# Filler matmuls at three places of each group in the attention layer of a two-layer graph network

## What is computed

```python
s_u = x @ W_u.T + b_u
s_v = x @ W_v.T
e = s_u[src] + s_v[dst]
e = jnp.where(e >= 0, e, 0.2 * e)
m = jax.ops.segment_max(e, dst, num_segments=n_nodes)
e_exp = jnp.exp(e - m[dst])
denom = jax.ops.segment_sum(e_exp, dst, num_segments=n_nodes)
msg = xh[src] * (e_exp / denom[dst])[:, None, :]
out = jax.ops.segment_sum(msg, dst, num_segments=n_nodes)
```

## Time and profile before

| | before |
|---|---|
| median of 3 runs | 4783.03 us (4782.73 to 4785.0) |
| the profiled execution's own time | 4782.31 us |
| its span, from the first to the last instruction | 4780.3 us |
| busy: PE, DVE, ACT, POOL | 65%, 38%, 26%, 70% |
| mean granted clock of TensorE | 0.801 |
| stretch of layer 1 in the span | about 3188 to 4570 us |

### The profile page before, as it was taken

The page is one execution under the profiler, slowest core; times in us unless marked ns, Lnnn a source line. Parts: engine busy times, 40 slices in busy tenths (PEclk is TensorE's granted clock), DMA queues, the critical chain, the costliest instruction groups (busy, mean ns, idle before and its releaser), DMA issues. The chain is left out here.

```text
span 4780.3 us, 63739 instructions
## 1 busy us (share of the span) xinstructions
PE 3085.9 (65%) x14137; PEld 1904.0 (40%) x14138; DVE 1818.5 (38%) x3829; ACT 1260.6 (26%) x4030; POOL 3344.6 (70%) x2982
## 2 busy tenths in 40 slices
PE   2568777777877777787778767844443444444446
PEld 1234444444444444444444434533332333333335
DVE  2543333333333333333333327853433433433325
ACT  0222222222222222222222223323333333333312
POOL 4248888888888888888888877985556555555545
PEclk7878998888888889889888989976666666666667
DMA  7687667666666666766766666645565565655553
GB/s 286 175 285 136 128 124 138 133 124 138 133 126 132 136 129 124 136 135 125 137 131 128 127 110 191 203 142 159 176 183 173 179 186 170 187 180 170 170 169 107
DMA packets 572820, 743.49 MB, mean 156 GB/s; under 512 B 184000, under 2 KB 467716, under 8 KB 568948
## 3 DMA queue, kind: packets, MB, share of 16 engines
q0 software_dynamic: 199136, 338.75, 37.3%
q1 hardware_dynamic: 351504, 363.52, 24.3%
q10 hardware_dynamic: 22148, 40.87, 2.7%
HBM read 441.65 MB, written 301.26 MB: 155 GB/s over the span
## 5 line engine op out<-in xcount | busy, mean ns | idle before, releaser
L814 POOL DMA_INDIRECT S<-l_msum,l_sink x784 | 1281.9, 1635 | 251.1 <-issue 219.1
L1316 POOL DMA_INDIRECT l_feats<-X_rows,l_gsrc x784 | 781.3, 997 | 571.7 <-PE l_psU L1373 269.8
L797 POOL DMA_INDIRECT l_ga<-A_rows,l_gsrc x784 | 790.3, 1008 | 259.4 <-issue 167.1
L887 PE MATMUL l_psU<-l_hid,l_same 128*128 128x257 f32 x1568 | 584.6, 458 | 540.3 <-ACT l_hid L923 527.5
L927 ACT COPY l_msum<-l_psU 128x257 f32<-128x257 f32 x784 | 292.6, 373 | 1880.4 <-POOLq L813 1361.0
L860 PE MATMUL l_psC<-l_table,l_onehot 128*128 x4728 | 721.9, 294 | 0.0
L1373 PE MATMUL l_psU<-l_feats,l_same 128*128 128x264 f32 x1568 | 516.5, 491 | 315.1 <-issue 173.9
L853 PE MATMUL l_psC<-W1cT,l_attrT 64*128 64x256 f32 x1576 | 618.7, 476 | 11.2 <-issue 11.2
L860 PEld LDWEIGHTS l_psC<-l_table,l_onehot 128*128 128x128 bf16 x4728 | 424.0, 103 | 363.3 <-issue 303.1
L1373 PEld LDWEIGHTS l_psU<-l_feats,l_same 128*128 128x128 f32 x1568 | 366.3, 244 | 444.2 <-issue 220.1
L887 PEld LDWEIGHTS l_psU<-l_hid,l_same 128*128 128x128 f32 x1568 | 264.5, 211 | 678.2 <-ACT l_hid L923 615.6
(11 more groups left out here) (305 smaller groups left out, 3658.4 us busy)
## 6 DMA issues: line engine op xcount, KB each, us to landing
PT<-l_part SPq DMA_DIRECT2D x196, 544.0 KB
l_srcb<-src_rows SPq DMA_DIRECT2D x99, 512.0 KB
S<-su_zeros ACTq DMA_DIRECT2D x24, 1156.5 KB
l_locb<-loc_rows SPq DMA_DIRECT2D x99, 256.0 KB
nd_sums<-S SPq DMA_DIRECT2D x196, 128.5 KB
l_attr<-in_edge_attr SPq DMA_DIRECT2D x98, 256.0 KB
l_locb<-loc_rows SPq DMA_DIRECT2D x49, 512.0 KB
GH_rows<-l_hidden SPq DMA_DIRECT2D x49, 384.0 KB
```

The lines of the kernel that those rows point to most:

```text
L797: pool.indirect_dma_start(ga[:, s, :], None, D["A"], bass.IndirectOffsetOnAxis(ap=gsrc[h][:, j % HALF:j % HALF + 1], axis=0)).then_inc(gat ...
L814: pool.indirect_dma_start(D[f"S{j % NTAB}"], bass.IndirectOffsetOnAxis(ap=sink[j // HALF][:, j % HALF:j % HALF + 1], axis=0), msum[:, j % ...
L887: nc.tensor.matmul(psU[j % 2][:, 0:UW], same[j // HALF][:, j % HALF, :], hid[:, j % RING, :], start=True, stop=True).then_inc(agg_done, 1)
L1316: pool.indirect_dma_start(feats[r][:, t, :], None, D["X1"], bass.IndirectOffsetOnAxis(ap=gsrc[r][:, t:t + 1], axis=0)).then_inc(gathered[r ...
```

## The change

Layer 1 gets a constant tile of zeros, `idle_in`, and the eighth PSUM bank, `idle_out`. PE multiplies the tile by itself, 128x128 by 128x512 in bf16, 12 times ahead of the wait for `scores_ready`, 4 times ahead of the wait for `max_ready` and 8 times ahead of the wait for `same_ready`: 24 more matmuls, each with its weight load, in every group. Nobody reads the result. DVE clears the tile once, ahead of its first instruction of the phase, and PE waits for that once. The number of buffer sets stays at two.

```diff
+        WARM = (12, 4, 8)
+        idle_in = m.sb("idle_in", [P, 512], BF16)
+        idle_out = m.ps("idle_out", [P, 512])
+        idle_ready = m.sem("idle_ready")
         @block.tensor
         def _(pe):
+            def keep_warm(count):
+
+                for _ in range(count):
+                    nc.tensor.matmul(idle_out[:, :], idle_in[:, 0:P], idle_in[:, :], start=True, stop=True)
+
+            pe.wait_ge(idle_ready, 1)
             dst_scores(0, 0, 0)
             dst_scores(0, 0, 1)
             def body(g, r, u, last):
+                keep_warm(WARM[0])
                 pe.wait_ge(scores_ready, g + 1)
...
                 if not last:
                     dst_scores(g + 1, (r + 1) % SETS, 0)
+                keep_warm(WARM[1])
                 pe.wait_ge(max_ready, g + 1)
...
                 if not last:
                     dst_scores(g + 1, (r + 1) % SETS, 1)
+                keep_warm(WARM[2])
                 pe.wait_ge(same_ready, g + 1)
...
+            nc.vector.memset(idle_in[:, :], 0.0).then_inc(idle_ready, 1)
             for r in range(SETS):
                 stage_index(r, r)
```

## The result

| | before | after |
|---|---|---|
| median | 4784.01 us (4782.73 to 4788.07) | 4848.03 us (4844.45 to 4852.91) |
| span of the profiled execution | 4780.3 us | 4842.4 us |
| mean granted clock of TensorE | 0.801 | 0.826 |

The ratio is 1.0133, with an interval from 1.0115 to 1.0151: the change makes the kernel slower by 64 us. The forecast of 4710 us was wrong, in direction too, and 4848 lies outside its range.

A forecast was written before the change was run, and what follows sets the result against it. Layer 1's period was taken as ACT's sixteenth copy, slowed during POOL's gathers, plus the chain to the next aggregation, with PE waiting. 4782.3 - 87 (gain) + 12 (late fillers) + 2.3 (start and end) = 4710 us, range 4645 to 4820.

The forecast's parts named there:

- Price of a filler: On PE, one 512-column bf16 matmul takes 0.22 us at 2.4 GHz and 0.44 at 1.2 GHz.
- The clock: PE's clock rises while the eight fillers run, near the aggregation's first tile; 0.5 us cost in 25 groups, 12 us.
- Rival B: Clock stays low through the eight fillers ahead of the aggregation, putting them on the path: 4841 us; 0.27 together with C.
- The copies: ACT's aggregate copies: tenth near +6, 13 to 14 done before the slow stretch, sixteenth at +14 to +17, not +20.8.
- POOL's stream: POOL has all tiles released and doesn't pause: 16 gathers at 1.25 us from +1.65 end at +21.4.
- From the stream to the aggregation: DVE's subtraction 1.6 us after POOL's last gather, aggregation 1.9 later: +24.9, period 25.8 with 0.9 us for slow gathers.
- The twelve ahead of the scores: Between aggregation and transposes, 2.6 to 5.3 us of PE, covered by 5 us of waiting: no cost, +2 us once.
- The gain: Layer 1's period falls from 27.65 to 25.8 us: 1.85 us for 47 groups, 87 us.
- rival A: ACT's gain is handed on to POOL within two groups: 0.77 us per group, 4760 us, or 4782 if nothing is left; 0.15.
- Rival D: No effect: clock rises but ACT's sixteenth copy stays tied to the stretch's end, 4775 to 4790 us; 0.13.
- Rival C: With three tiles open on PE, POOL never pauses, scores turned after its stream: 28.8 us period, 4837; 0.27 with B.
- Wrong in the main if the slow stretch isn't tied to POOL's stream: Stated failure condition: then an early ACT would bring the period to 20 us, or nothing would move.

The follow-up runs named there:

- e8: Changed kernel without the twelve fillers ahead of the scores, against the kernel before on a chip of the first kind: 4781.62 us, ratio 0.9999.
- e14: Changed kernel with POOL waiting ahead of its fifth gather until the next group's scores are turned, against the kernel before, first kind: 4705.36 us, ratio 0.986.
- e1: Changed kernel without the twelve fillers ahead of the scores, against the kernel before on a chip of the second kind: 4562.12 us, ratio 0.9999.
- e5: Changed kernel run again unaltered, against the kernel before on another run's chip of the first kind: 4871.82 us, ratio 1.0182.

## Why the prediction was wrong, point by point

*Price of a filler:* right. Twelve at full clock take 2.75 us, 0.23 each (0.22 taken); eight at half clock 3.57, 0.45 each (0.44 taken). The four ahead of the maximum cost nothing, as said: they end at 3373.45, 7.1 us ahead of its transpose.

*The clock:* right for the aggregation, 0.90 to 1.00 from the first tile on. It didn't rise while the eight last fillers ran, as I had taken it to: they had 0.50 throughout, and still the aggregation follows the subtraction by 2.06 us, against 1.94: the 0.5 us charged in 25 groups, 12 us in all, weren't there, only 0.12 of it. Rival B, slower because of a clock that stays at half, did not happen; its 4841 us are near the result by another way.

*The copies:* right. The tenth at +5.9 (forecast near +6), fourteen ahead of the break (13 to 14), the sixteenth at +13.3 (+14 to +17).

*POOL's stream:* right. The last gather ends at +21.9 (forecast +21.4 for 16 gathers without a pause).

*From the stream to the aggregation:* this step failed, and it alone turns the sign. I took 1.6 us from the end of the stream to the subtraction, and 1.9 from there. Measured: 2.7 us from the end of the stream to the copy of the *turned scores*, then the whole 5.3 us chain (5.45 here) to the aggregation: 21.9 + 2.7 + 5.4 = 30.0 in place of 24.9 (25.8 with the 0.9 us for slow gathers). The subtraction, forecast 1.6 us after POOL's last gather, comes 6.1 us after it. The 1.6 us came from one group, of which I had read only the maximum. Its scores were held too:

```profile
3410.65 0.42 PE L1358 MATMUL l_psE<-ident,l_start 128*128 128x128 f32 x1
...
3422.98 0.37 ACT L1395 COPY l_turned<-l_psE 128x256 f32<-128x256 f32 x1 [3.70 <-DMA block_words<-su_word_i]
```

ACT got them 12.3 us after the transpose, with POOL streaming, but 5.6 us before the stream's end. So the first steps of the chain lay beside the stream, and only the subtraction and what follows it stood behind. In the changed kernel the transposes stand at +10.4, inside the stretch, the scores come only after the stream, and the whole chain stands behind it. This is the group shown; in the layer it varies: of the 47 copies that come over 2 us after their transpose, half follow POOL's last ended gather by 2.6 us or more, a quarter by less than 1.

*The twelve ahead of the scores:* priced at nothing "as long as ACT's copies end as late as they do", and up to 2 us where ACT ends early, "another limit is longer then". But they move a hand-over across the edge of the stretch, and so the cost isn't their 2.7 us. (0, 4, 8) at 0.9999 beside (12, 4, 8) at 1.0182 on one chip shows that all of the loss depends on them. That the cover of an edit is a wait which the same change shortens by 7.5 us is what I should have followed to its end.

*The gain:* the forecast 87 us for full clock didn't come even without the twelve, 0.9999. The account of e8 has 150 us less at the aggregates than its kernel before, and 80 more at each of the other two waits. This is rival A, the gain handed on within a pair of groups, at its weakest end (4782). Rival D named nearly that time too, but not by what happened: its sixteenth copy was to stay tied to the end of the stretch, and in the changed kernel it comes at +13.3, with the stream's end at +21.9.

*Rival C* gave nearly the right time, 28.8 us for a group and 4837 us, by the right mechanism: POOL never pauses, the scores are turned for ACT only when the stream ends. Measured 30.0 in the group shown and 1382.4 / 48 = 28.8 on average. Its condition was too narrow: it asked for three open tiles on PE when the stretch starts; PE had none open, the twelve fillers did it. It had 0.27 together with B, and deserved more: the forecast needed turned scores that pass during an unbroken stream, and the one such group that I had looked at had them 12.3 us late.

*"Wrong in the main if the slow stretch isn't tied to POOL's stream":* it is tied to it on the first kind (e14). What the trace of one chip could not show is that four other chips don't have the stretch; there the change is worth nothing, as far as its variants show.

Left open: (12, 4, 8) itself was not run on the second kind, and (12, 0, 0) not on the first, so whether the twelve cost by themselves or only together with the full clock isn't settled. Nor is it whether the kernel before gains by the pause on the first kind.

## What to carry to other kernels

When a change moves a hand-over in time, check what the trace shows for hand-overs in the place that it moves to, and not only whether the waiting time there covers the added work. A kernel whose slowest waits lie beside a stream of indirect gathers may gain from pausing the stream at the hand-over, on a chip that has the effect, and loses on one that hasn't: here -1.4% and +2.0 to 2.2% from the same edit. A gain of the size of 1% should be looked at on more than one chip before it is kept.

## What the runs showed of the hardware

The same program takes 4773 to 4784 us on chips of the first kind and 4558 to 4562 on four of the second, 4.6 to 5.0% apart. Most of the difference lies in layer 1. With (0, 4, 8) on both kinds (e8, e1) the spans are 206 us apart; the exponentials, first to last start, take 1299.6 and 1146.1 us, which is 153 of it. Another 39 us lie ahead of the first exponential, and 14 behind the last.

The load on the DMA engines alone doesn't make it. In the stretch of the changed kernel they are busy for 0.73 at 211 GB/s (the window of 3365.20 above). In e1, with no stretch, nearly the same:

```profile
3526.00:3540.60 14.60, 3.86 (x40) 2.26 (x42) 5.92 (x11) 1.78 (x4) 11.56 (x11) 0.60 0.66 212
```

Nor is it POOL's pace: a gather with nothing on DVE beside it takes 0.95 us and follows the last by 1.25 on both kinds. What differs is how long a finished matmul needs to be known to another engine: from the start of the second transpose to ACT's copy 14.2 us in the changed kernel and 0.46 us in e1, both with POOL streaming. The trace's records of semaphore updates say the same of the whole layer: from the start of the second transpose to the update are at most 0.43 us in each of the 49 groups of every run on the second kind, and 12.7 us in the median of the 48 groups of the changed kernel that have the record.

PE itself is slowed too. The four fillers ahead of the maximum wait for nothing and tell nobody, and yet in the group above they come apart:

```profile
3368.99 1.01 PE L1345 MATMUL l_idle_out<-l_idle_in 128*128 128x512 bf16 x2
3370.75 0.59 PE L1345 MATMUL l_idle_out<-l_idle_in 128*128 128x512 bf16 x1 [0.75 <-issue]
3372.86 0.59 PE L1345 MATMUL l_idle_out<-l_idle_in 128*128 128x512 bf16 x1 [1.53 <-issue]
```

In 23 of the 49 groups (29 in e5) one of the four starts over 1 us after the one ahead of it; in the runs with (12, 4, 8) on the second kind the distance is 0.43 us at most.

The Trainium skill (Perfetto Trace Analysis, Tensor Engine Instruction) says that a matmul's end in the profile is an estimate from its size, and that the semaphore update is pushed only after PSUM has acknowledged the write, and takes its way after that. No run here tells which of the two, the acknowledgement or the way, is slow, but it fits that no matmul's own row shows the 14 us: the views have them as idle time of the engine that waits, under the name of a DMA that has nothing to do with it. The spread fillers, which update no semaphore, speak against the way of the update as the only slow part. The stretch isn't strictly bound to the end of the stream either: in e8 ACT took the scores at 3618.37 with POOL's last two gathers still to come. What is different in the two kinds of chip stays open.
